# Asking for a batch's similarity rows two batches ahead instead of one, in a fused conv + expert kernel

## The reference

```python
# similarity-modulated convolution with three taps
sim = [cos(emb, emb shifted right), cos(emb, emb), cos(emb, emb shifted left)]   # over channels, per position
att = jnp.repeat(sim, C, axis=1)
inp_unf = jnp.stack([f_pad[:, :, k:k + T] for k in range(3)], axis=2).reshape(B, C * 3, T)
out = jnp.einsum('bit,oi->bot', inp_unf * att, w_flat)
# block
x = x + tanh(g_xattn[0]) * conv(_layernorm(x), ctx, weight)
x = x + tanh(g_ffn[0]) * experts(_layernorm(x))      # 8 experts of rank 16, the top 2, gates over their sum
```

## Time and profile before

| | |
|---|---|
| median of 3 runs | 290.56 us |
| lowest, highest | 289.19, 295.38 us |
| profiled execution, its own time | 292.49 us |
| its span in the profile | 290.6 us |
| mean granted PE clock | 0.906 of full |
| busy share PE, DVE, POOL, ACT | 77, 56, 54, 50% |

### The profile page before, as it was taken

How to read it: one execution, slowest core, us unless ns; L and a number is a source line. 1 busy time by engine, 2 the same in 40 slices (tenths; PEclk the granted TensorE clock), 3 DMA queues, 4 the chain that set the end, 5 groups by cost and what they waited for, 6 DMA issues and landing times.

```text
span 290.6 us, 3919 instructions
## 1 busy us (share of the span) xinstructions
PE 224.7 (77%) x1110; PEld 144.7 (50%) x1110; DVE 162.4 (56%) x403; ACT 146.0 (50%) x253; POOL 157.1 (54%) x280
## 2 busy tenths in 40 slices
PE   7887787995996962968769798297867858988972
PEld 5632344673644441745554544165545545656651
DVE  1589557871753621775557344286645546659553
ACT  3989472963662643174548245326453636445020
POOL 1655394665771764064739366406464636765541
PEclk9999799799597896699979869779997989999999
DMA  7994060501150160121203012012121201101113
GB/s 240 341 382 169 0 218 2 218 13 67 74 188 36 73 223 3 74 77 76 77 17 136 6 72 78 4 72 78 76 79 74 76 36 49 76 7 72 72 74 144
DMA packets 9568, 27.97 MB, mean 96 GB/s; under 512 B 1965, under 2 KB 2600, under 8 KB 9548
## 3 DMA queue, kind: packets, MB, share of 16 engines
q1 hardware_dynamic: 9548, 27.73, 25.9%
HBM read 18.67 MB, written 8.39 MB: 93 GB/s over the span
## 4 chain that ended last, share of the span: by engine, by line
PE 35%; issue 20%; DVE 20%; SPq 14%; ACT 5%; DMA 4%; POOL 1%; DVEq 0%; POOLq 0%; ACTq 0%
SPq L312 12%; DVE pt L715 8%; PE bank L941 6%; PE bank L916 5%; DMA rows<-rows 4%; PE bank L920 3%; DVE x L722 3%; PE bank L934 3%; PE bank L921 3%; PE bank L897 3%; PE bank L922 3%; PE bank L857 2%; DVE x L759 2%; DVE pr L633 2%; ACT unread L521 2%
## 5 line engine op out<-in xcount | busy, mean ns | idle before, releaser
L402 POOL TENSOR_TENSOR pt_lo<-pt,pt_hi 128x512 fp32r<-128x512 f32 x60 | 79.2, 1337 | 100.0 <-ACT pt_hi L537 89.0
L715 DVE TENSOR_TENSOR pt<-xn,bank 128x512 f32<-128x512 f32 x96 | 63.2, 679 | 87.1 <-issue 60.9
L537 ACT ACTIVATE pt_hi<-pt 128x512 fp32r<-128x512 f32 x60 | 37.0, 630 | 78.9 <-DVE pt L715 78.8
L941 PEld LDWEIGHTS bank<-aT,xT 128*128 128x128 f32 x256 | 40.7, 223 | 12.3 <-ACT xT L543 6.3
L941 PE MATMUL bank<-aT,xT 128*128 128x136 f32 x256 | 42.3, 317 | 1.6 <-ACT xT L543 1.3
L916 PE MATMUL bank<-pt,wT 128*128 128x512 f32 x72 | 39.9, 636 | 0.0
L543 ACT ACTIVATE xT<-bank 128x512 f32<-128x512 f32 x32 | 18.9, 589 | 27.9 <-PE bank L934 27.8
L920 PE MATMUL bank<-pt_hi,w_hi 128*128 128x512 f32 x60 | 32.0, 534 | 0.0
L897 PE MATMUL bank<-rows,sel 9*128 9x512 bf16 x72 | 10.1, 413 | 25.7 <-DMA rows<-rows 25.7
L921 PE MATMUL bank<-pt_lo,w_hi 128*128 128x512 f32 x60 | 26.5, 441 | 0.0
L922 PE MATMUL bank<-pt_hi,w_lo 128*128 128x512 f32 x60 | 26.3, 438 | 0.0
(11 more groups left out here) (101 smaller groups left out, 352.9 us busy)
## 6 DMA issues: line engine op xcount, KB each, us to landing
et<-ctx SPq DMA_DIRECT2D x16, 512.0 KB, 5.7
xt<-x SPq DMA_DIRECT2D x16, 512.0 KB, 3.3
out<-x SPq DMA_DIRECT2D x15, 512.0 KB, 2.6
rows<-rows SPq DMA_DIRECT2D x108, 6.0 KB
aT_in<-expert_aT SPq DMA_DIRECT2D x1, 544.0 KB, 7.9
bm_in<-expert_b SPq DMA_DIRECT2D x1, 512.0 KB, 10.6
out<-x SPq DMA_DIRECT2D x2, 256.0 KB, 2.0
sel<-select SPq DMA_DIRECT2D x1, 216.0 KB, 7.8
```

Source lines behind the costliest of these rows:

```text
L402: nc.gpsimd.tensor_tensor(pt_lo[:, i, :], pt[:, i, :], pt_hi[:, i, :], ALU.subtract).then_inc(lo_done, 1)
L537: nc.scalar.activation(pt_hi[:, i, :], pt[:, i, :], ACT.Copy).then_inc(hi_done, 1)
L715: nc.vector.tensor_tensor(pt[:, i, :], xn[:, n % 2, h * HALF + t:(h + 1) * HALF + t], sim_bank(k)[:, :], ALU.mult).then_inc(mod_done, 1)
L941: last = nc.tensor.matmul(h_ps[:, 0:ER + E], xT[:, n % 2, c, :], aT[:, c, :], start=(c == 0), stop=(c == KC - 1))
```

## The change

In loop n SP asks for the rows of batch n + 2 in place of n + 1. The number and shape of transfers, their slots and all waits inside `load_rows3` stay as they are. The first request, for batch 4, is now in loop 2; the last, for batch 15, in loop 13.

```diff
-                if ABREAST <= n + 1 < B:
-                    load_rows3(n + 1)
+                if ABREAST <= n + 2 < B:
+                    load_rows3(n + 2)
```

## The result

The changed kernel takes 259.96 us, median of 4 runs (259.13 to 260.52), against 290.34 us for the kernel before in the same session (4 runs); the ratio is 0.896, 95% interval 0.893 to 0.899. The kernel before has a slower state too, near 295 us in some executions; all ratios leave these out, the medians quoted for it do not. The forecast was 257.5 us with a range of 252.5 to 266. The profiled execution took 259.8 us, span 258.0, mean granted clock 0.954 (before 0.906).

The account below looks back on a forecast made before the run. The bound was taken to be a ring through SP's queue issuing row transfers behind the residual's x load. Removing 25.7 us of waits and 9.0 of half clock takes 292.49 profiled to 257.8; forecast 257.5 us, range 252.5 to 266.

Parts of the forecast that it names:

- The ring: Residual, x load, nine issues, landing, PE's spreads, DVE products, taps, residual; asking earlier removes all ten L897 waits, 25.7 us.
- The exceptions, batches 4, 8 and 12: Rows written in the loop that asks for them (2, 6, 10), so SP waits: cost 0, upper bound 15 us.
- The loops: Pairs from loops 3 and 4 to 11 and 12, rebuilt from loop 13/14's 11.75 us: 145.5 us against 180.18.
- the 1.1 us in the sum: DVE's context product L633 in loops 3, 4, 7 and 8, fully exposed through PE's wait at L950: 1.1 us each.
- The sum: Loops 3 to 12 at 145.5 us against 180.18: saved 34.7 us, 25.7 of waits and 9.0 of half clock.
- half clock: PE at its lower level, 1.2 GHz, after standing idle in the row waits: 9.0 us saved with them.
- POOL becomes the bound: Rival, chance 0.12: POOL's L402 pair, slowed beside DVE's L633, holds loops 3, 4, 7 and 8; 261 us.
- Only the waits go: Rival, chance 0.15: other gaps still drop PE to its lower clock, only 25.7 us saved; 265 us.
- More comes back: Rival, chance 0.10: DVE's product hidden, and clock also back in loops 5 and 9; about 250 us.
- The slower side: Rival, chance 0.02: SP held to the loop's end delays next x load and store; +11, 302 us.

Follow-up runs that it names:

- The experiment that held SP longest: Changed kernel, but from batch 6 the request for batch n + 2 waits until batch n + 1's second spreads are done: 266.19 us, ratio 0.917.

## Why the prediction was right

*The ring and its removal.* Right in place and size. All ten waits for the rows went, 25.7 us; SPq L312 left the chain. That the residual's x load was the link that mattered is shown by putting the rows ahead of it; that the rest of the ring is worth what its parts sum to is shown by closing it again (12.68 us a loop).

*The exceptions, batches 4, 8 and 12.* Right at 0. In loop 6 the rows were issued from 5.2 us into the loop, SP was free again at 11.4, and the x load of the next loop went out at 14.2 when its residual came. Loop 10 is the same. For loop 2 compare the x loads of loops 1 and 3: 36.70 and 64.02 before, 38.03 and 65.30 after, 27.3 us apart in both.

*The loops.* Rebuilt from loops 13 and 14 they were to be 27.8, 33.4, 27.8, 33.0 and 23.5 us; they are 28.7, 32.7, 28.2, 32.95 and 23.6, in sum 146.2 against 145.5. A miss of 0.9 and one of -0.7 cancel in part in it. The waits of 1.5 us at L950 in loops 3, 4, 7 and 8 came as forecast, but the reason given for the 1.1 us in the sum ("for exactly that DVE queue", so "all of it is exposed") was only half of it: ACT's square lay beside DVE's product, and moving the product alone gave nothing.

*The clock, and luck in the number.* This is the term that was mis-sized. The sum has 9.0 us of half clock beside 25.7 us of waits. For the profiled execution of before that was so: its loops took 180.18 us, those of the changed kernel 146.20, 34.0 less. But filling the waits gave the median back only 4.4. With that figure the sum is 290.2 less 25.7 less 4.4, or 260.1; measured 259.6 and 260.0. The step that failed is the one from the profiled execution (292.49) to the median. The full 34.7 us taken off the median of 290.56 would have been 255.9, 4.1 too low; the recorded 257.5 stands close to what was worked out for the profiled execution, 257.8, though that execution lay 1.9 above the median, and no reason is given for it. So the forecast came within 2.5 us in part by luck.

The sum against the profiled execution's own time, 257.8, ended at 259.8. Of these 2.0 us, 0.7 is the loops and 1.3 is the start, where the first x load of loop 3 left at 65.30 and not 64.02. That is no effect of the change: the x load of loop 1 already left 1.33 us later (38.03 against 36.70), and the first request that the change moves is in loop 2. In ten profiled executions of the edited kernels and of the changed one again the x load of loop 3 left between 64.3 and 66.6. The profiled execution of the kernel before thus had the earliest start of all twelve and was still 2 us above its median, so what made it long lies behind the start. This is a second sign that its 180.18 us are not typical.

*The rivals.* The measured 260.0 lies nearer to the number of "POOL becomes the bound" (261) than to the forecast, but its mechanism did not happen. POOL's timeline in loop 3 of the changed kernel shows the longer pair behind idle time:

```profile
72.33 3.37 POOL L402 TENSOR_TENSOR pt_lo<-pt,pt_hi 128x512 fp32r<-128x512 f32 x2 [1.46 <-ACT pt_hi L537]
```

It is as long beside DVE's product as in the earlier trace rows, and the 1.46 us in front of it took that up. The kernel with the product moved had the shorter pair and the same time. "Only the waits go" (265) was wrong: the clock rose to 1.00 in three of the five pairs. But of the 9.0 us by which it differs from the sum, the median had only about half. "More comes back" (250) did not happen by itself; the kernel with ACT's copy moved reached that time, 249.96. The slower side did not happen. The experiment that held SP longest, which is nearest to it, cost 6 us and not 42 (302 against 260), as stores and x loads up to 4 us late found no one waiting.

## What to carry to other kernels

When a queue that only issues transfers stands at the head of the chain, ask for each issue what it waits for by position and not by data: here nine small transfers stood behind a load that waited for a result they had no use for, and moving them either one place up or one batch ahead gave the same 30 us. Work that an engine does behind a wait, though its inputs are there already, belongs in front of it; the copies, products and squares moved so gave 13 us more. Size such changes from a loop in the same trace that lacks the wait, and take small terms from medians of several executions: two single ones gave twice the clock's share.

## What was not expected of the hardware

Time and mean granted clock do not go together from one execution to the next of the same kernel: of the executions of the kernel before that stood beside these runs, one took 290.2 us at 0.905 and one 291.9 us at 0.929. A term for the clock that is read off one trace can therefore be off by some us; this one was off by 4.6 (9.0 against 4.4).

The clock fell behind a wait of under 2 us. PE's timeline in loop 8 of the kernel before:

```profile
164.10 0.39 PE L897 MATMUL bank<-rows,sel 9*128 9x512 bf16 x3 [1.94 <-DMA rows<-rows]
...
165.22 1.84 PE L941 MATMUL bank<-aT,xT 128*128 128x136 f32 x8
```

After 1.94 us of idle the eight L941 take 1.84 us against 1.09, the low level of 1.2 GHz for most of them: the granted clock is 1.00 until 165.2, 0.60 in the next microsecond and 0.50 in the one after. The waits of 1.50 us at L950 in loops 3 and 4 of the changed kernel left the level at 1.00. But the length of the wait does not decide by itself. In the kernel with ACT's copy moved, PE has the same three short waits in loop 5 (0.35, 0.36 and 0.77 us, from 103.15 to 106.19) and in loop 9 (0.36, 0.37 and 0.75 us, from 159.53 to 162.57). Behind the first the clock falls: it is 0.50 from 108 to 110 us, and four transposes L936 take 1.06 us against 0.60. Behind the second it stays at 1.00, and the pair is 0.2 us shorter. What decides is not shown by these runs.

The issue of one row transfer of 6 KB (three partitions) holds SP for 0.64 to 0.72 us in the changed kernel, about twice the 0.33 us (median; 0.33 to 0.50) of an x load of 512 KB. So the bytes do not set SP's time here; whether it is the shape or that both ends lie in SBUF was not separated.
